# The plain attention code placed ahead of the guarded one, in a one-core attention and expert kernel

## The reference

```
x = x + layernorm(attn(layernorm(x)))        # 16 batches of 256 tokens, 128 channels, 8 heads
    qn, kn = norm(qq), norm(kq)              # per head
    fid = (qq @ kq.T) / maximum(qn * kn, EPS_COS)
    aw  = 0.5 * fid * (1 + 0.1 * sin(pi * fid)) + 0.5 * (Q @ K.T) / sqrt(HD)
    heads = softmax(aw) @ V                  # then the projection, two layernorms and a small feed-forward
x = x + layernorm(experts(layernorm(x)))     # gate, argmax, gelu(x @ w1[e] + b1[e]) @ w2[e] + b2[e]
```

## Time and profile before

| | |
|---|---|
| median of 3 runs | 484.68 us (482.29 to 484.83) |
| span of the profiled execution, first to last instruction | 480.7 us |
| the profiled execution's own time outside the span | not given; the median lies 3.98 us above the span |
| PE busy | 370.3 us, 77% |
| DVE busy | 366.4 us, 76% |
| ACT busy | 321.6 us, 67% |
| prologue / attention / rest, read from the timeline | 0 to 58 / 58 to 273 / 273 to 481 us |

### The profile page before, as it was taken

How to read it: one execution, slowest core, us unless ns; L and a number is a source line. 1 busy time by engine, 2 the same in 40 slices (tenths; PEclk the granted TensorE clock), 3 DMA queues, 4 the chain that set the end, 5 groups by cost and what they waited for, 6 DMA issues and landing times.

```text
span 480.7 us, 9097 instructions
## 1 busy us (share of the span) xinstructions
PE 370.3 (77%) x2782; PEld 264.4 (55%) x2782; DVE 366.4 (76%) x895; ACT 321.6 (67%) x612; POOL 235.5 (49%) x340
## 2 busy tenths in 40 slices
PE   0977458999999999999898799775010899999960
PEld 0755335566666666666555532645000699999950
DVE  5587559999999999999995434499798238867771
ACT  1347416999999999999985545666520666777630
POOL 7458307555555555555220203100547728887773
PEclk9997856999999999999987999997655699999995
DMA  8507531667776677667839990000103968987400
GB/s 206 22 0 168 124 99 43 166 169 169 168 168 167 166 170 166 169 168 168 182 100 135 142 135 12 1 1 1 35 28 86 288 188 231 248 242 206 112 16 0
DMA packets 87084, 60.86 MB, mean 127 GB/s; under 512 B 16189, under 2 KB 79681, under 8 KB 87030
## 3 DMA queue, kind: packets, MB, share of 16 engines
q1 hardware_dynamic: 79814, 54.69, 52.2%
q0 software_dynamic: 2496, 4.29, 2.6%
q10 hardware_dynamic: 4720, 1.25, 1.3%
HBM read 35.90 MB, written 25.21 MB: 127 GB/s over the span
## 4 chain that ended last, share of the span: by engine, by line
DVE 50%; PE 20%; issue 11%; POOL 10%; ACT 5%; DMA 2%; POOLq 0%; DVEq 0%; SPq 0%; ACTq 0%
DVE big L1826 13%; DVE mxs L1803 12%; POOL out_dram L842 6%; DVE big L1856 5%; POOL fst L835 2%; PE ps L1608 2%; PE ps L1205 2%; PE ps L1413 2%; PE ps L1505 2%; PE ps L1510 2%; DVE arena L2234 1%; DVE u_sb L1865 1%; DVE arena L2238 1%; DVE gb L1674 1%; ACT big L959 1%
## 5 line engine op out<-in xcount | busy, mean ns | idle before, releaser
L1803 DVE TENSOR_REDUCE mxs<-ps 128x4 f32<-128x1024 f32 x64 | 74.0, 1217 | 6.7 <-PE ps L1240 6.7
L1826 DVE SCALAR_TENSOR_TENSOR big<-big,ps 128x1024 f32<-128x1024 f32 x64 | 74.0, 1215 | 3.6 <-ACT big L949 3.6
L949 ACT ACTIVATE big<-ps 128x1024 f32<-128x1024 f32 x64 | 62.4, 1028 | 9.3 <-PE ps L1378 9.1
L828 POOL DMA_INDIRECT sorted_rows<-proj,sl_i x32 | 32.9, 1027 | 51.4 <-issue 43.7
L842 POOL DMA_INDIRECT out_dram<-arena,fidx x46 | 46.7, 1014 | 15.8 <-issue 10.5
L1608 PE MATMUL ps<-arena,big 128*128 128x256 f32 x184 | 46.0, 395 | 0.6 <-ACT arena L1147 0.6
L747 POOL CAST mtok<-mxs 128x16 bf16<-128x16 f32 x16 | 3.1, 197 | 87.1 <-DVE mxs L1803 87.1
L1240 PE MATMUL ps<-arena 96*128 96x256 bf16 x256 | 39.5, 284 | 7.3 <-issue 4.7
L1620 PE MATMUL ps<-big,arena 128*128 128x128 f32 x368 | 44.8, 275 | 0.0
L1620 PEld LDWEIGHTS ps<-big,arena 128*128 128x128 f32 x368 | 42.9, 192 | 0.3 <-ACT arena L1156 0.3
L1856 DVE TENSOR_TENSOR big<-big,ps 128x1024 f32<-128x1024 f32 x32 | 37.8, 1216 | 2.4 <-PE ps L1400 2.4
(11 more groups left out here) (347 smaller groups left out, 856.7 us busy)
## 6 DMA issues: line engine op xcount, KB each, us to landing
big<-in_L_ffn_w_dram SPq DMA_DIRECT2D x42, 256.0 KB, 3.4
qk_parts<-proj SPq DMA_DIRECT2D x16, 384.0 KB, 2.8
arena<-qk_parts SPq DMA_DIRECT2D x32, 192.0 KB, 3.7
sorted_rows<-zrow SPq DMA_DIRECT2D x16, 266.0 KB, 5.8
arena<-qk_parts SPq DMA_DIRECT2D x32, 128.0 KB, 3.9
x_all<-sorted_rows SPq DMA_DIRECT2D x23, 133.0 KB, 3.1
sorted_rows<-zrow SPq DMA_DIRECT2D x2, 1263.5 KB, 25.6
sorted_rows<-zrow SPq DMA_DIRECT2D x2, 1197.0 KB, 22.0
```

The source lines that it names most:

```text
L949: nc.scalar.activation(W[par][:, n, :], src, ACT.Sin, scale=PI * (1 - 1e-6)).then_inc(sin_ready, 1)
L1803: nc.vector.tensor_reduce(mxs[:, b1 % 2, :, 2 * n:2 * n + 2], src, AX_X, ALU.max, negate=True).then_inc(unit_free, 1)
L1826: nc.vector.scalar_tensor_tensor(W[par][:, n, :], W[par][:, n, :], 10.0, f, ALU.add, ALU.mult).then_inc(unit_free, 1)
```

## The change

The condition is turned around, so that the plain version is the first of the two blocks and the guarded one the second. The code behind attention becomes a function `rest`, which is called where both meet; its contents are the same. No instruction that computes, no wait and no DMA is added, removed or reordered within a version.

```diff
-        def either(eng, body):
+        def either(eng, body, rest):
 
             eng.wait_ge(flag_ready, 1)
             v = eng.value_load(flag[0:1, 0:1], min_val=0, max_val=1)
-            with eng.If(v != 0):
-                batches(eng, body, True)
-            with eng.Else():
+            with eng.If(v == 0):
                 batches(eng, body, False)
+            with eng.Else():
+                batches(eng, body, True)
+            rest()
...
-            either(pe, body)
-
-
-            pe.wait_ge(h_done, NB + 1)
+            def rest():
+                pe.wait_ge(h_done, NB + 1)
...
+            either(pe, body, rest)
```

More of the change, by code:

```diff
@@ L987, in body @@
                     heads_out(b)
[L989 to L1004, removed]
@@ L1020, in turn_qe @@
[L1020 to L1034, removed]
@@ L1036, in wide_square_t @@
[L1036 to L1155, removed]
-                    nc.scalar.activation(fg[par][:, c, :], ps[:, 1 + 2 * par + c // 2, (c % 2) * TS:(c % 2 + 1) * TS], ACT.Gelu,
-                                         bias=bias[:, c:c + 1]).then_inc(fs["g"], 1)
@@ L1185, in _ @@
+            either(act, body, rest)
         @block.tensor
@@ L1473, in body @@
                     heads_back(b)
-            either(pe, body)
-            pe.wait_ge(h_done, NB + 1)
-            def gate_x(g):
-                h = g // GH
-                return nc.tensor.matmul(ps[0:64, 2 + h, :], gw_at[:, g % GH, :], xnT[:, g * GT * P:(g + 1) * GT * P],
-                                        start=(g % GH == 0), stop=(g % GH == GH - 1), skip_group_check=True)
-            def turn_gates(h):
-                pe.wait_ge(step["xg"], 4 * h + 2)
-                for i in range(GT):
-                    mm = nc.tensor.transpose(ps[:, 2 + h, i * 64:(i + 1) * 64], gx_s[:, i * P:(i + 1) * P], ident[0:64, 0:64])
-                mm.then_inc(step["xg"], 1)
@@ L1491, in ytile @@
-            def ytile(t):
-                return y_of(t // GT)[:, (t % GT) * P:(t % GT + 1) * P]
-            def turn(g):
-                if g:
-                    pe.wait_ge(step["aT"], g)
-                for i in range(GT):
-                    mm = nc.tensor.transpose(ps[:, 0, i * P:(i + 1) * P], u_sb[:, g * GT + i, :], ident[:, :])
-                mm.then_inc(step["at_ps"], 1)
-            def out_proj(g):
-                pe.wait_ge(step["aT"], g + 1)
-                if g:
-                    pe.wait_ge(step["y"], g)
-                nc.tensor.matmul(ps[:, 1, :], wo_c[:, :], aT[g % 2], start=True, stop=True).then_inc(step["y_ps"], 1)
@@ L1507, in of_y @@
-            def of_y(g):
-                first, last = g % GH == 0, g % GH == GH - 1
-                pe.wait_ge(step["y"], g + 1)
-                nc.tensor.matmul(ps[0:32, 2 + g // GH, :], wA_at[:, g % GH, :], y_of(g),
-                                 start=first, stop=last, skip_group_check=True)
-                pe.wait_ge(step["ysq"], g + 1)
-                nc.tensor.matmul(ps[32:64, 2 + g // GH, :], mean_at[:, g % GH, :], ysq[g % 2],
-                                 start=first, stop=last, skip_group_check=True).then_inc(step["p1"], 1)
@@ L1530, in second_sum @@
-            def second_sum(g):
-                pe.wait_ge(step["qeT"], g + 1)
-                for i in range(GT):
-                    o = zregion(g, i)
-                    if g >= 2 and i % 2 == 0:
-                        pe.wait_ge(step["t"], 2 * (g - 2) + i // 2 + 1)
-                    nc.tensor.matmul(o, ytile(g * GT + i), M1[:, :], start=True, stop=False)
-                    mm = nc.tensor.matmul(o, qeT[g % 2], MB[:, i, :], start=False, stop=True)
-                mm.then_inc(step["z_ps"], 1)
@@ L1540, in _ @@
-            turn(0)
-            for g in range(NG + 1):
-                if g + 1 < NG:
-                    turn(g + 1)
-                if g < NG:
-                    out_proj(g)
-                if g == GH + 1:
-                    turn_acc(0)
-                if g == 1:
-                    pe.wait_ge(set_cp, 3)
-                if g:
-                    of_y(g - 1)
-            def count_rows(h):
-                pe.wait_ge(rsem["p"], 2 * h + 1)
-                m = rt[:, 0, h * TH:(h + 1) * TH, :].rearrange("p t e -> p (t e)")
-                nc.tensor.matmul(ps[:, 2 + h, 0:TH * NE], ones[:, :], m, start=True, stop=True)
-                nc.tensor.matmul(ps[:, 2 + h, TH * NE:2 * TH * NE], tri_m[:, :], m, start=True, stop=True).then_inc(rsem["p"], 1)
@@ L1558, in _ @@
-            pe.wait_ge(step["q8"], 1)
-            gate_x(0)
-            gate_x(1)
-            turn_acc(1)
-            turn_qe(0)
-            turn_qe(1)
-            gate_x(2)
-            gate_x(3).then_inc(step["xg"], 1)
-            second_sum(0)
-            turn_qe(2)
-            second_sum(1)
-            turn_gates(0)
-            turn_qe(3)
-            second_sum(2)
-            second_sum(3)
-            turn_qe(4)
-            turn_qe(5)
-            pe.wait_ge(step["q8"], 2)
-            for g in range(GH, NG - 1):
-                gate_x(g)
@@ L1578, in _ @@
-            gate_x(NG - 1).then_inc(step["xg"], 1)
-            second_sum(4)
-            turn_qe(6)
-            second_sum(5)
-            turn_qe(7)
-            turn_gates(1)
-            count_rows(0)
-            second_sum(6)
-            second_sum(7)
-            count_rows(1)
-            def list_out():
-                pe.wait_ge(rsem["x"], 1)
-                for k in range(2):
-                    mm = nc.tensor.matmul(ps[0:1, 5, k * P:(k + 1) * P], tile_list[:, k:k + 1], ident[:, :], start=True, stop=True)
-                mm.then_inc(rsem["x"], 1)
@@ L1613, in f_down @@
-            def f_down(s):
-                par = s % 2
-                if s >= 3:
-                    pe.wait_ge(fs["z"], s - 2)
-                pe.wait_ge(fs["g"], (s + 1) * EC)
-                for t in range(RS):
-                    for c in range(EC):
-                        mm = nc.tensor.matmul(ps[:, 5 + s % 3, t * C:(t + 1) * C], fg[par][:, c, t * P:(t + 1) * P], fw2[s % DEPTH][:, c, :],
-                                              start=(c == 0), stop=(c == EC - 1))
-                mm.then_inc(fs["y_ps"], 1)
@@ L1976, in logits @@
-            def logits(h):
-                lo, lw = lx[:, 0, h * TH:(h + 1) * TH, :], lx[:, 1, h * TH:(h + 1) * TH, :]
-                dve.wait_ge(step["rc"], 2 * h + 2)
-                chain(nc.vector.tensor_tensor(T(10, h), T(11, h), T(5, h), ALU.mult))
-                chain(nc.vector.tensor_tensor(lw, lw, T(5, h).unsqueeze(2).to_broadcast([P, TH, NE]), ALU.mult))
-                chain(nc.vector.tensor_tensor(lo, lo, lw, ALU.add))
-            def add_shift(g):
-                dve.wait_ge(step["rb"], 2 * (g // GH) + 2)
-                for i in range(GT):
-                    t = g * GT + i
-                    s1 = nc.vector.scalar_tensor_tensor(u_sb[:, t, :], u_sb[:, t, :], tl[:, 3, t:t + 1], be2c_bc[:, :], ALU.mult, ALU.add)
-                s1.then_inc(step["s1"], 1)
@@ L2126, in _ @@
-            chain(nc.vector.reciprocal(std0[:, :], mv_all[:, 1, :]))
-            for g in range(GH + 2):
-                first_sum(g)
-            var_y(0)
-            first_sum(GH + 2)
-            angle(0)
-            first_sum(GH + 3)
-            fold(0)
-            queries(0)
-            var_y(1)
-            weigh(0)
-            angle(1)
-            fold(1)
-            times_x(0)
-            weigh(1)
-            sum_t(0)
-            weigh(2)
-            queries(1)
-            times_x(1)
@@ L2186, in _ @@
-            newton(4, 5, step["rc"], 1)
-            dots(1)
-            var_by_parts(1)
-            logits(1)
-            best(1)
-            newton(6, 7, step["rd"], 1)
-            weight_in(1)
-            add_shift(2)
-            add_x(2)
-            places(1)
-            weight_out(1)
-            for g in (GH - 1, GH):
-                add_shift(g)
-                add_x(g)
-            list_tiles()
-            for g in range(GH + 1, NG):
-                add_shift(g)
-                add_x(g)
@@ L2251 @@
+            either(dve, body, rest)
 _INS = ['L0_attn_x', 'L0_attn_Wq', 'L0_attn_bq', 'L0_attn_Wk', 'L0_attn_bk', 'L0_attn_Wv', 'L0_attn_bv',
```

968 lines of the change are left out of this document (628 added, 340 removed).

## The result

| | median | runs |
|---|---|---|
| before | 484.80 us (482.29 to 486.53) | 14 |
| changed | 487.51 us (485.18 to 490.33) | 14 |

The ratio is 1.0061 with a 95% interval of 1.0040 to 1.0081: slower by 2.7 us, a little more than the 0.5% that can be told. The profiled execution of the changed kernel is the slowest of its 14 (490.33 us, which is its span and 1.7 us); if the same 1.7 lies around before's span of 480.7, that execution took 482.4, near before's fastest. So the two spans, 7.9 us apart, show more than the medians: 5.2 us of them are the luck of the two executions.

The account below looks back on a forecast made before the run. DVE was taken to bound attention's start, PE the passage behind its last batch. −5.45 + 8.9 + 0.5 = +3.95 on the 480.7 us span, plus 3.98 to the median, gave 488.6 us; range 481.5 to 492.5.

Parts of the forecast that it names:

- The entry: Start of attention: falling through removes DVE's 5.85 us idle before its third maximum; gain 5.45 us after a deduction.
- the allowance of 0.4: At attention's start: 0.4 us taken off the gain because maxima return later in a fuller queue; bounds 0 and 1.5.
- The exit: Behind the last batch: PE, ACT and DVE now jump to the rest, whose code must be fetched; loss 8.9 us.
- the upper price: Jump behind attention: zero fill delays PE's code fetch, making the jump 10.0 us long; loss 8.9 rather than 2.4 us.
- one late packet: Instruction packet at 269.04 under the zero fill, read as 103 PE instructions late, 6.5 us later than the others.
- The last term, 1.4 us: PE's jump behind attention: 1.4 us from the instruction packet's end until PE goes on, as at attention's start.
- Rival 1: Behind attention: an awaited fetch starts at once, so the jump costs 2.4 to 2.9 us; 482.1 us, chance 0.19.
- The price of the clock: PE behind attention: a longer pause may lengthen the half-clock stretch; 0.5 us taken, bounds 0 and 3.
- A jump that costs nothing: Behind attention: no loss a fetch could explain, only the 5.45 us gain; 479.2 us, chance 0.04.
- An entry that brings nothing: Attention's start: branch stalls taken or not, or the maxima's transfer takes the gain; 493.7 us, chance 0.07.
- ACT adds nothing: Behind attention: ACT's copy follows PE's turn by 0.7 us, so its jump adds nothing unless q14 is slower than q8.
- The 3.98 us between span and median: Whole kernel: the median 484.68 lies 3.98 us above the profiled span 480.7; carried over to the forecast.

Follow-up runs that it names:

- once more: The changed kernel, unaltered, measured and profiled a second time: 488.21 us against 483.37 for the kernel before, ratio 1.0104.

## Why the prediction was right

The range, 481.5 to 492.5, held the time (487.51 against 488.6), the sign was right, and the mechanism was the one that was named. Term by term, each column is the difference of one profiled execution from the one of the kernel before; the places are the flag, DVE's weighing of the second batch (87.18 before, 81.61 in the changed kernel), its last product of attention, PE's first turn of the rest and DVE's first sum:

| stretch | predicted | changed | once more |
|---|---|---|---|
| up to the flag | 0 | −0.94 | −1.11 |
| flag to second batch | −5.45 | −4.63 | −5.33 |
| second batch to last product | 0 | +1.96 | +0.91 |
| last product to PE's turn | +8.9 | +9.54 | +9.06 |
| PE's turn to first sum | +0.5 | +0.47 | +0.47 |
| first sum to the end | 0 | +1.49 | +0.27 |
| span | +3.95 | +7.89 | +4.27 |

**The entry.** DVE's wait was the fetch of its own code, and falling through costs nothing that shows, as taken. The maxima left as soon as SP was done with its loads, as the prediction had it; counted from the flag they left 3.1 us earlier and not 2.57, since the six loads ahead of them took 2.6 us instead of 3.7, and PE didn't wait for them. The 0.6 us that went missing between the first weighing (5.26 ahead) and the second batch (4.63) are DVE's wait for PE's softmax logits, 1.51 us where it was 0.86 before; the allowance of 0.4 covered it by chance. The flag's own shift isn't the change's: it lies between 55.65 and 57.05 in all eleven traces, in no order that goes with the edits. And the price itself was read from one execution: in the second trace of the same code the idle time is 7.33 us, so the 5.45 holds for one execution and not for each.

**The exit.** The step that carried the forecast was to take the upper price, from one late packet inside the stretch. It gave 7.0 us until the packet starts and 10.0 for the jump; measured were 8.1 and 10.95, 7.3 and 10.47, and with PE alone 9.81, with a packet at 4.5 and another at 7.1. The last term, 1.4 us from the packet's end until PE goes on, held in every jump (1.4 to 1.7). That the late fetch was the fill's doing is borne out by the run without the fill there, but the size has luck in it: the 240 instructions between fetches were the mean of five counts from 217 to 308, and against the 258 of that run the fetch was 85 late, an estimated 5.6 us, by which the same steps give a loss of about 8. Rival 1, a fetch that starts at once, is what happens where no fill runs at the jump: where it is moved away (3.59 us), and where it pauses or runs out (3.89 and 4.06). By the Trainium skill, page "Runtime: NRT & Kernel Launch", section "Instruction fetch mechanics", a taken branch to a target outside the two pages held waits for a DMA fetch of that page; each of PE's jumps in these traces agrees, from 3.54 to 10.95 us, with a packet on q8 inside it.

**The clock.** The price of the clock was read from rows, but the choice of 0.5 us between 0 and 3 had none, and 0.47 came: PE's first turn of the rest ran at half clock, for 1.12 us instead of 0.66. That the choice fit so well is luck.

**The rivals.** A jump that costs nothing (479.2) is refuted by the two versions without a jump in the way, 478.17 and 479.68, which are what that rival would have been. An entry that brings nothing (493.7) is what the change on PE alone measures, 493.10. That ACT adds nothing held in the changed kernel, where its copy waits for PE; with PE spared, its jump and DVE's cost as much as the entry brings.

**What was off.** The 3.98 us between span and median are not time outside the span: each execution whose span and time are both known shows 1.7 to 1.8 us there. The other 2.3 say that the profiled execution of before was near its fastest. As a forecast of the median, 484.68 + 3.95, the sum is right to carry them over, and the medians of the two comparisons (+2.7 and +4.8) lie on both sides of the +3.95; but the rows that its terms were read from are those of a fast execution.

And the forecast let DVE's head start reach the exit whole. It doesn't: in the first trace (with the flag's own shift in it) it is 5.7 us at batch 14, 4.8 at batch 15 and 3.6 at the last product; in the second 6.4, 5.4 and 5.5, lost in batch 14 alone. In that place PE's clock was at half, 1.2 GHz, once more often than before, which is what the second run was expected to show. Windows of the changed kernel, then of the last fill in turns:

```profile
226.00:230.00 4.00, 4.00 (x37) 1.82 (x30) 3.79 (x5) 2.93 (x5) 1.64 (x3) 0.57 0.78 153
```

```profile
226.00:230.00 4.00, 3.76 (x42) 2.75 (x42) 4.00 (x5) 3.75 (x6) 0.94 (x2) 1.00 0.75 169
```

With the clock at 1.00 a window of the same length holds 42 of PE's matmuls instead of 37. Seven of the eleven traces have a slow stretch of 3.4 us in batch 14: within 224 to 231 both of the changed kernel, the one without a guard, the rest in both blocks and the four fills one by one; from 232.6 the kernel before with the fill moved; and from 234.1 the change on PE alone. Each of them loses 0.9 to 1.1 us there against the trace of before, which has none. So this loss is not the change's: the code of before shows it too, in one of its two traces. The two runs with the fill behind the exit or in turns have no such stretch and carry 6.3 of 6.4 us to the exit. What decides whether the clock falls there is open. The last row of the table isn't the change's either: from the first sum to the end, the ten other traces lie 0.1 to 1.9 us above this one of before, in no order that goes with the edits.

## What to carry to other kernels

Code that never runs has a price by its place: it is paid where an engine jumps over it, so a branch's blocks are laid out by what waits at each of their ends, not by which one is likelier. If the jump can't be avoided, put it at the end of an engine's program, or keep long queues of DMA away from the moment it is taken; here these two turned a loss of 0.6% into gains of 0.9% and 0.65%. And look at every engine that jumps: with PE spared, ACT and DVE came back late and set the pace.

## What the runs showed of the hardware

- The same jump of PE takes 3.54 to 3.67 us with the DMA engines quiet and 9.81 to 10.95 under the queued zero fill; the packet behind whose end PE goes on starts 1.0 to 1.2 us behind the branch in the one case and 7.1 to 8.1 in the other. From the packet's end until PE goes on it is 1.4 to 1.7 us in both.
- A branch's record doesn't show its stall on every engine. PE's is as long as the stall; ACT's and DVE's are 38 to 72 ns while they stand still for 6 to 10 us, which the timeline calls "issue" or puts down to another engine.
- Sixteen fills in turns instead of four at once moved 88 GB/s instead of some 140, with pauses between them, and the packets took 32 ns each instead of 78.
